# A four-layer block in one program: experts on all tokens, or on routed tokens gathered by indirect DMA

## The reference, cut to what matters

```python
def _L0_ffn_ref(hidden_states, classifier_w, e_score_correction_bias, gate_w, up_w, down_w):
    x = hidden_states                                   # layer norm of the residual, 2048 x 256
    logits = jnp.einsum('bsh,eh->bse', x, classifier_w) # 12 routes: 8 experts, 4 "zero" routes
    probs = jax.nn.softmax(logits, axis=-1)
    biased = probs + e_score_correction_bias
    _, idx = jax.lax.top_k(biased, 2)
    rw = jnp.take_along_axis(probs, idx, axis=-1) * 1.5
    w_full = jnp.sum(jax.nn.one_hot(idx, total) * rw[..., None], axis=-2)
    g = jnp.einsum('bsh,eih->bsei', x, gate_w)          # 8 experts, 128 inner channels
    u = jnp.einsum('bsh,eih->bsei', x, up_w)
    act = jax.nn.silu(g) * u
    expert_out = jnp.einsum('bsei,ehi->bseh', act, down_w)
    out = jnp.einsum('bse,bseh->bsh', w_full[..., :8], expert_out)
    return out + x * jnp.sum(w_full[..., 8:], axis=-1, keepdims=True)
```

## Time and profile before

| | before |
|---|---|
| median of 3 runs (lowest, highest) | 837.68 us (835.0, 838.4) |
| profiled execution, first to last instruction | 832.7 us |
| busy share: TensorE, VectorE, ScalarE, GpSimd | 90%, 74%, 49%, 69% |
| `routed_experts` and its route choice | 170.9 to 349.2 us |
| `latent_attention` | 349.2 to about 743 us |
| DMA traffic | 24.12 MB, mean 29 GB/s |

### The profile page before, as it was taken

The page is one execution under the profiler, slowest core; times in us unless marked ns, Lnnn a source line. Parts: engine busy times, 40 slices in busy tenths (PEclk is TensorE's granted clock), DMA queues, the critical chain, the costliest instruction groups (busy, mean ns, idle before and its releaser), DMA issues. The chain is left out here.

```text
span 832.7 us, 14911 instructions
## 1 busy us (share of the span) xinstructions
PE 750.6 (90%) x4808; PEld 535.8 (64%) x4808; DVE 615.8 (74%) x1115; ACT 406.6 (49%) x1084; POOL 570.9 (69%) x589
## 2 busy tenths in 40 slices
PE   4999999859999999689999999999999999866785
PEld 2555555447878877556777777777777777543454
DVE  5898999868887878665565576886678667749995
ACT  1688888533322322216454544555454445444453
POOL 5667776326676757564657778787878887716976
PEclk9999999989999999999999999999999999998999
DMA  9200000040000010122110000000000000000011
GB/s 262 103 1 0 0 0 1 2 168 20 20 19 20 19 57 0 57 95 96 48 49 1 1 1 1 3 1 1 1 1 2 1 2 1 1 2 7 25 33 38
DMA packets 8763, 24.12 MB, mean 29 GB/s; under 512 B 1711, under 2 KB 5167, under 8 KB 8087
## 3 DMA queue, kind: packets, MB, share of 16 engines
q1 hardware_dynamic: 8154, 23.28, 8.5%
q10 hardware_dynamic: 549, 0.08, 0.1%
HBM read 21.26 MB, written 2.10 MB: 28 GB/s over the span
## 5 line engine op out<-in xcount | busy, mean ns | idle before, releaser
L1606 POOL TENSOR_TENSOR q<-turned 64x512 f32<-64x512 f32 x128 | 168.0, 1313 | 23.5 <-DVE turned L1532 9.5
L1283 PE MATMUL ps<-l_yt,a 128*128 128x512 f32 x576 | 144.1, 400 | 2.1 <-ACT p L1429 1.6
L1283 PEld LDWEIGHTS ps<-l_yt,a 128*128 128x128 f32 x576 | 104.9, 188 | 26.9 <-issue 4.7
L1593 POOL TENSOR_TENSOR p<-p,l_inverse 128x512 f32<-128x512 f32 x64 | 66.8, 1047 | 77.3 <-DVE l_inverse L1554 76.9
L1429 ACT ACTIVATE p<-ps,l_negmax 128x128 f32<-128x128 f32 x256 | 91.1, 382 | 43.1 <-DVE l_negmax L1523 43.1
L1532 DVE TENSOR_TENSOR turned<-ps,rope 128x1024 f32<-128x1024 f32 x64 | 78.0, 1220 | 42.4 <-PE ps L1283 39.8
L871 PE MATMUL ps<-yt_experts,wsplit 128*128 (+1 forms) x384 | 97.3, 403 | 5.7 <-DVE h L974 5.2
L467 DVE TENSOR_REDUCE negmax<-ps 128x4 f32<-128x512 f32 x128 | 84.4, 685 | 13.3 <-PE ps L290 12.8
L871 PEld LDWEIGHTS ps<-yt_experts,wsplit 128*128 128x128 f32 x384 | 71.2, 192 | 23.1 <-issue 5.4
L1523 DVE TENSOR_REDUCE l_negmax<-ps 128x4 f32<-128x512 f32 x64 | 41.2, 686 | 45.8 <-PE ps L1341 45.6
L383 ACT ACTIVATE pt<-ps 128x512 f32<-128x512 f32 x128 | 71.2, 599 | 6.8 <-PE ps L312 4.5
(11 more groups left out here) (213 smaller groups left out, 1571.1 us busy)
## 6 DMA issues: line engine op xcount, KB each, us to landing
wide<-in_wide SPq DMA_DIRECT2D x8, 768.0 KB, 4.5
mx_raw<-in_mx SPq DMA_DIRECT2D x8, 384.0 KB, 3.1
x<-in_x SPq DMA_DIRECT2D x4, 512.0 KB, 8.4
ctx_t<-in_ctx_t SPq DMA_DIRECT2D x1, 2048.0 KB, 7.8
out<-x SPq DMA_DIRECT2D x16, 128.0 KB, 1.7
narrow<-in_narrow SPq DMA_DIRECT2D x8, 192.0 KB, 2.7
ktraw<-in_ctx_rows SPq DMA_DIRECT2D x1, 1248.0 KB
wraw<-in_gate SPq DMA_DIRECT2D x1, 1024.0 KB, 18.1
```

What stands on the lines that cost most here:

```text
L1283: out = pe.matmul(tile_bank(n, k), a[i][:, pa, kin, k * 128:(k + 1) * 128], yt[j % 2][:, py, kin, :, :].rearrange("p b s -> p (b s)"), sta ...
L1593: pool.tensor_tensor(p[:, head, :, :], p[:, head, :, :], spread(inverse[:, head, :], 2, S), ALU.mult).then_inc(normed[head], 1)
L1606: t = pool.tensor_tensor(out[rows[(head + half) % 2], head, :], turned[rows[head], half, :], turned[rows[head], 2 + half, :], ALU.add)
```

## The change

The experts are computed on routed tokens alone, in tiles of 128 slots. The steps are:

1. While rows are normalised for the routes, SP stores them to a DRAM table `token_rows` (6 pairs in `grouped_attention`, 2 in `turn_rows`).
2. After the route choice the slots are counted on chip: matmuls with a triangle give each token's rank in its expert, every expert gets whole tiles, and 40 tiles hold any outcome. One-hot matrices (`at_place`, `at_tile`, `of_pick`) and 32 matmuls turn picks into the list of tokens by slot.
3. GpSimd gathers 128 rows a tile by indirect DMA, 8 tiles ahead at most. 20 steps of two tiles each follow: turn the rows (4 transposes), gate and up (12 matmuls of 256 columns), turn h (2 transposes), down (6 matmuls of 256 columns). The tile's expert is a register read from SBUF (`value_load`), which selects the weights' columns.
4. The results go to a DRAM table `slot_rows`. For each group of 4 sequences 8 indirect DMAs fetch them back, and VectorE adds them to x with the route weights. Group 0 is done at the end of the stage, groups 1 to 3 inside the first steps of `latent_attention`, where GpSimd also waits until the rows have landed.
5. 8 of the 16 chunks of the last layer's weights are quantised in this stage, the other 8 in steps 8 to 23 of `latent_attention`.
6. The zero routes' part of x is applied by 16 ScalarE activations, ahead of the first tile's rows on that engine.
7. Semaphores are held to the end of the program, except those of `grouped_attention`, which are cleared after it with one more barrier of all engines.

```diff
+            pe.matmul(sums_ps, used, m.ones16[:, :], start=True, stop=True).then_inc(summed, 1)
+            pe.matmul(ranks_ps, tri, used, start=True, stop=False)
...
+            for a in range(PICKS):
...
+                t = pe.matmul(tokens_ps, at_place[:, a, :], of_pick[:, a, :], start=(a == 0), stop=(a == PICKS - 1))
+            for n in STEPS:
+                find_columns(n + 1)
+                turn_rows_of(n + 1)
+                turn_gated(n - 1)
+                gate_and_up(n)
+                down(n - 1)
+                if turn_in(n) is not None:
+                    mx.turn(pe, m, turn_in(n), mx_ps)
...
+            act.wait_ge(affine, 4)
+            act.wait_ge(routed.rows_stored[3], 32)
+            for n in range(B):
+                act.activation(m.x[:, n, :], m.x[:, n, :], ACT.Identity, bias=offset[:, n, :],
+                               scale=factor[:, n, :]).then_inc(x_scaled, 1)
+            keep_rows(0)
+            for n in STEPS:
+                keep_rows(n + 1)
+                keep_gated(n - 1)
+                gates(n)
+                keep_out(n - 1)
...
+            def gather(tile):
+                if inside(tile, SLOT_TILES):
+                    wait(pool, y_turned, tile // 2 - GATHERS // 2 + 1)
+                    pool.indirect_dma_start(y[tile % GATHERS], None, routed.rows[:, :],
+                                            bass.IndirectOffsetOnAxis(ap=r.token[:, tile:tile + 1], axis=0)
+                                            ).then_inc(gathered[tile % GATHERS], 16)
...
+            for tile in range(GATHERS):
+                gather(tile)
+            pool.wait_ge(total_made, 1)
             pool.tensor_tensor(factor[:, :, 0], r.total[:, :], m.rstd[:, :, 0], ALU.mult).then_inc(affine, 1)
...
+            for n in STEPS:
+                rotate(ROTARY_STEPS + n)
+                for t in range(2):
+                    gather(GATHERS + 2 * n + t)
+                if powers_in(n) is not None:
+                    mx.divide(pool, powers_in(n))
+                if shift_in(n) is not None:
+                    mx.multiply(pool, shift_in(n))
+            for i in range(STORES):
+                pool.wait_ge(stored[i], 16 * (TILE_STEPS // STORES))
...
+            for k in range(TOP_K):
+                routed.fetch(pool, 0, k, rows_in_slots)
```

and in GpSimd's loop of `latent_attention`:

```diff
                 add(n)
+                if group_in(n, 3) is not None:
+                    deviations(group_in(n, 3))
+                for k in range(TOP_K):
+                    if group_in(n, k) is not None:
+                        routed.fetch(pool, group_in(n, k), k, rows_in_slots)
+                        routed.wait_fetched(pool, group_in(n, k), k)
+                if chunk_in(n, 0) is not None:
+                    mx.divide(pool, chunk_in(n, 0))
+                if chunk_in(n, 1) is not None:
+                    mx.multiply(pool, chunk_in(n, 1))
```

748 lines of the change are left out of this document (457 added, 291 removed).

## The result

The changed kernel takes 887.59 us in the median of its runs (883.84 to 889.34), the kernel before 838.04: a ratio of 1.0594, interval 1.0558 to 1.0629. It is slower, as forecast, but by 50 us and not by 9, and outside the range of 816 to 880. The profiled execution has a span of 884.3 us against 832.7.

A forecast was written before the change was run, and what follows sets the result against it. TensorE was taken to bound the experts and the latent attention. The first latent matmul 11.0 us earlier and 20.0 us more in the latent attention gave +9.0 on the 832.7 us span, hence 846.7 us; range 816 to 880.

The forecast's parts named there:

- (d): Latent attention: eight weight chunks cost 2.7 us of TensorE turns and, with VectorE's work mostly hidden, 2.3 us more.
- g: GpSimd's time for issuing one indirect DMA of 128 rows, put at 1.2 us; each 0.1 us worth 6.1 together.
- cheap: Rival, chance 0.24: g = 0.7, so TensorE bounds the experts' steps and the change wins, at 819 us.
- level: Rival of no difference, chance 0.20: g = 1.04, giving 836.9 us.
- slow gathers: Rival, chance 0.08: g = 2.0, costing 49 us more, 896 us.
- 20 steps and the last tile: Experts: 16 steps at GpSimd's 4.8 us, four at TensorE's 4.2, together 93.6; the last tile 3.7.
- TensorE's registers: Rival, chance 0.12: two register loads per experts' step stop TensorE's queue for 2.6 us; 26 us more, 873.
- From the last copy to the first latent matmul: Experts' tail: copy, store landing, eight fetches (9.6 us), additions and statistics, ending at the first latent matmul at 338.2.
- (a): Start of the latent attention: TensorE is cold after more than 20 us of idling, costing 3.0 us.
- (b): Latent steps 0, 1, 3, 4, 6, 7: GpSimd's four fetches and wait take 7.0 us each; 10 us lost.
- (c): Latent steps 2, 5, 8: VectorE's additions and statistics, 5.5 us, mostly hidden, cost 2 us; 16 without that cover.
- Clock: TensorE's granted clock: 0.50 at the starts of experts and latent attention, adding 2.0 and 3.0 us.

The follow-up runs named there:

- e1: The changed kernel without any work on the eight weight chunks in the latent stage; 847.1 us.
- e9: The changed kernel with VectorE's latent chunk operations moved between a step's second maximum and its first rotation; 892.1 us.
- e7: The changed kernel with ScalarE's sixteen scalings of x put one in each of the experts' steps 3 to 18; 874.3 us.
- e14: The changed kernel with TensorE's two register loads of a step moved ahead of the down product; 884.7 us.
- e8: The changed kernel without fetch and combine of groups 1 to 3 in the latent stage; 861.7 us.
- e5: The changed kernel with GpSimd's wait for its four fetches moved behind the next step's two normalisations; 879.5 us.
- e12: The changed kernel with one full-width VectorE operation in place of the five of a latent chunk's shift, mantissas unrounded; 851.4 us.
- e17: The changed kernel with latent chunks every three steps, not two, their nine VectorE operations split 4, 3 and 2; 862.9 us.

## Why the prediction was wrong, step by step

The step that failed is (d) of the latent attention, "VectorE gets 3.3 us a chunk, beside 6.4 in 10.8, which hides them except where the front of the feed-forward falls into the same step", 5.0 us for eight chunks. They cost 38 us (e1: 1.0594 to 1.0137). The 3.3 us are prices of operations alone: nine operations take 3.4 us in e9 and 8.6 in the changed kernel. The earlier trace rows held the warning: the rounding operation takes 0.55 us alone and up to 1.54 beside GpSimd. I used that for the token list (1.5 us) and in the experts' steps, and not in the latent steps, where GpSimd's five additions stand side by side and VectorE has six or seven such operations per chunk, at the end of the step, just ahead of the maxima that open the next. The shift of five takes 6.5 us in the step shown, of which, by my estimate, some 3 are free.

- *g = 1.2.* Right: one issue every 1.25 us, 0.95 of work and 0.30 between. With that the rivals that hang on g, cheap, level and slow gathers, fall: an issue's price did not decide. (The range names 816 as the cheap gathers' end; their own sum is 819. Nothing hangs on it.)
- *Token list at 196.8.* It was at 200.2. VectorE's first instruction of the route choice ran 3.4 us later (175.5 for 172.1), where 0.4 was allowed for; from there the chain took 24.7 us, for 24.3 in the sum.
- *First gate product at 217.4.* 220.9, late by what the list was late, and held by ScalarE's sixteen scalings as said; e7 confirms it.
- *20 steps and the last tile, 93.6 + 3.7 = 97.3 us.* 88.0, from 220.9 to 308.9, at 4.3 to 4.9 a step, and not set by GpSimd alone: the last steps, without gathers, are no shorter (turns of gathered rows at 291.16, 295.67 and 300.07).
- *TensorE's registers.* The loads leave a gap of 0.8 to 1.0 us in each step (0.8 forecast, 2.6 in the rival), but taking it away gives almost nothing (e14).
- *From the last copy to the first latent matmul, 23.9 - 3.7 = 20.2 us.* 22.8, 308.9 to 331.7: the first fetch waits for the last store until 312.55. In all the first latent matmul is 17.5 us earlier, 11.0 forecast.
- *(a), 3.0 us for the cold start.* The first latent matmul comes 17.5 us earlier and step 0 only 15.2: the 2.3 between them fit this term. TensorE is busy for 13.6 us there, for 10.9 before, at clock 0.81 for 1.00. By e8 steps 0 to 8 hold nothing more of it (105.2 us for 105.5).
- *(b) and (c), 10 + 2 = 12 us in steps 0 to 9.* 24.4 in steps 0 to 8. GpSimd's full steps were rightly foretold, and e5 shows it; the size was not. I let the first pair of fetches be free, and steps 0 to 2 took 29.2 us, for 26.0 before and 26.5 in e8. I gave VectorE's combine 2 us, where shortening it is worth 4.6 in these steps. The eight operations of a combine are again of the kind that waits for GpSimd: 0.86 us each, 0.48 alone. This does not add up to the whole of the 12 that are missing; the rest stays open.
- *Clock.* Foretold for the two starts, where the windows show it (0.50 and 0.54 while TensorE idles ahead of them). Not foretold: it falls in the latent steps too when TensorE has many gaps (0.94 in steps 8 to 24 with 25.0 us of waiting, 1.00 in e1 with none and in e12 with 3.7). That may be up to 11 of the 38.9 us: TensorE is busy for 191.1 us there and for 179.8 in e12, which has the same matmuls; how much of the 11 the waits would have hidden is not known.

The largest thing that the sum left out is thus one mechanism: VectorE's price per operation beside GpSimd, above all for the chunks and in part in the combine. That the kernel would be slower was forecast, but by GpSimd's issues; the greater part of the 50 us has another reason.

## What to carry to other kernels

Before moving work to an engine with free time, look at which operations it will stand beside, and price each small SBUF operation on VectorE, of the kinds that were stretched here, at the length of the GpSimd instruction that runs there, even if it is much smaller. Compare the sum of one step with what is free in that step, ahead of the operation that opens the next one; a mean over the stage hides it. Where such work must stay, fewer operations or the same ones spread thin cost a fraction: 0.8 us a chunk with five operations (e12, which leaves the rounding out, so it is a price and not a solution), 1.9 with nine in three steps (e17), 4.9 with nine in two.

## What the runs showed of the hardware

- A VectorE `tensor_scalar` or `scalar_tensor_tensor` on SBUF of 12, 16 or 384 columns mostly takes 1.2 to 1.5 us in a row beside GpSimd additions of 1.3 us, 0.17 to 0.56 alone; the first of a row mostly takes 0.6 to 0.9, and now and then one gets through in its own 0.17. A reduction, a reciprocal and batch statistics are not stretched (0.55, 0.23, 0.41 us). GpSimd seems to pay a little too: four additions took 5.55 us in the step shown, 5.26 in e5's.
- An indirect DMA of 128 rows of 1 KB costs GpSimd 1.25 us, and the first pair was on TensorE 4.4 us after the first issue (200.47 to 204.90).
- Two register loads leave TensorE idle for 0.8 to 1.0 us in a step of the experts; behind the gate and up matmuls that idle time is gone (e14).
